# A graph layer's edge loop, its body thirty chunks long instead of six

## What is computed

```
h_fwd, h_rev = h @ W_forward.T, h @ W_reverse.T            # 64 numbers per node each
messages = h_fwd[src] * direction[:, 0:1] + h_rev[src] * direction[:, 1:2]
scores = leaky_relu(einsum('ef,hf->eh', messages, attn_forward[0]), 0.2)     # 4 heads
exp_scores = exp(scores - scores.max(axis=0))
norm = exp_scores / (segment_sum(exp_scores, dst)[dst] + 1e-10)
outs = [segment_sum(messages * norm[:, hd:hd + 1], dst) for hd in range(4)]
...
x = x + gnn(layernorm(x), edge_index, edge_attr_2, ...)
x = x + ffn(layernorm(x)[None], ...)[0]
```

## Time and profile before

| | |
|---|---|
| time, median of 3 runs | 2498.59 us (2497.01 to 2499.44) |
| the profiled execution | 2504.92 us, its span 2503.1 us |
| mean granted TensorE clock of it | 0.924 |
| busy PE, DVE, POOL | 2162.4, 1958.6, 1608.8 us |

### The profile page before, as it was taken

One profiled execution on the slowest core, in us unless ns is written; L12 is line 12 of the kernel. 1 busy time (PEld: TensorE's weight loads), 2 busy tenths in 40 slices (PEclk: granted clock), 3 DMA queues, 4 the chain that ended last, 5 costly groups with the idle time before them and its releaser, 6 DMA issues.

```text
span 2503.1 us, 46180 instructions
## 1 busy us (share of the span) xinstructions
PE 2162.4 (86%) x12873; PEld 1868.6 (75%) x12874; DVE 1958.6 (78%) x4609; ACT 357.4 (14%) x1034; POOL 1608.8 (64%) x1725
## 2 busy tenths in 40 slices
PE   7598989899898989999898999999946589999970
PEld 6487878778787877878787787878736478888870
DVE  5797888888788878888888887888848856666657
ACT  4100000000000000000000000000016434444435
POOL 6676767676676767667676766767746753333327
PEclk9699999999999999999999999999955599999995
DMA  6232222222222222223222222222245676666657
GB/s 206 58 69 61 68 61 67 61 67 63 61 67 61 67 60 67 62 61 67 61 67 61 67 63 61 68 61 67 61 133 164 215 215 200 197 199 199 199 168 266
DMA packets 175493, 259.46 MB, mean 104 GB/s; under 512 B 46538, under 2 KB 120479, under 8 KB 174972
## 3 DMA queue, kind: packets, MB, share of 16 engines
q0 software_dynamic: 52672, 119.37, 19.5%
q1 hardware_dynamic: 122556, 136.70, 18.0%
HBM read 218.01 MB, written 38.81 MB: 103 GB/s over the span
## 4 chain that ended last, share of the span: by engine, by line
PE 41%; DVE 31%; issue 16%; DVEq 6%; DMA 3%; SPq 1%; ACT 1%; POOL 1%; ACTq 0%; POOLq 0%
PE p_hot L1007 31%; PE p_win L902 5%; DVE hot_ex L1072 4%; DVE p_hot L1122 4%; DVE p_part L1040 4%; DVE rows L1037 3%; DVEq L1772 3%; DVE onehot L1109 2%; DVE rows L1127 2%; DVE p_y L1995 1%; PE p_y L1940 1%; PE p_h L1930 1%; DVE hid_t L1967 1%; DVE second L1975 1%; DVE back L1980 1%
## 5 line engine op out<-in xcount | busy, mean ns | idle before, releaser
L280 POOL DMA_INDIRECT rows<-node_table,index x1343 | 1278.6, 952 | 506.6 <-issue 398.3
L1007 PE MATMUL p_hot<-parts,onehot 128*128 128x476 f32 x6160 | 1403.5, 388 | 75.7 <-issue 58.0
L1007 PEld LDWEIGHTS p_hot<-parts,onehot 128*128 128x128 f32 x6160 | 1170.8, 192 | 280.9 <-issue 73.5
L1122 DVE SCALAR_TENSOR_TENSOR p_hot<-place_no,place_of_source,p_hot 128x476 f32<-128x476 f32 x440 | 293.1, 711 | 98.9 <-PE p_hot L1007 98.9
L902 PEld LDWEIGHTS p_win<-hot_ex,msg 128*65 128x65 f32 x3136 | 201.8, 143 | 116.6 <-issue 113.3
L902 PE MATMUL p_win<-hot_ex,msg 128*65 128x64 f32 x3136 | 210.9, 227 | 87.4 <-DVE hot_ex L1072 86.3
L956 ACT ACTIVATE p_dve<-score,neg_shift 128x64 f32<-128x64 f32 x98 | 31.2, 318 | 1718.1 <-DVE score L1057 1718.1
L1781 POOL DMA_INDIRECT expert_rows<-ys,back x104 | 102.3, 983 | 269.3 <-DVE ys L2000 146.3
L1109 DVE TENSOR_TENSOR onehot<-key,p_dve 128x896 fp32r<-128x896 f32 x220 | 237.3, 1079 | 36.2 <-PE p_hot L1007 32.9
L1127 DVE TENSOR_REDUCE rows<-p_hot 128x136 f32<-128x952 f32 x220 | 252.8, 1149 | 7.7
L1023 DVE TENSOR_TENSOR shared<-shared,p_win 65x64 f32 x784 | 170.2, 217 | 111.8 <-PE p_win L902 16.0
(11 more groups left out here) (269 smaller groups left out, 1422.2 us busy)
## 6 DMA issues: line engine op xcount, KB each, us to landing
shared<-in_w SPq DMA_DIRECT2D x120, 512.0 KB, 4.5
rows<-node_table,index POOLq DMA_INDIRECT x1343, 3.0
xs<-dispatched SPq DMA_DIRECT2D x104, 129.5 KB, 4.1
shared<-expert_rows SPq DMA_DIRECT2D x12, 896.0 KB, 8.1
key<-hot_keys SPq DMA_DIRECT2D x62, 128.0 KB, 3.0
token_rows<-in_x SPq DMA_DIRECT2D x7, 896.0 KB, 12.8
key<-hot_keys SPq DMA_DIRECT2D x32, 192.0 KB, 3.1
shared<-in_x SPq DMA_DIRECT2D x7, 768.0 KB, 9.1
```

The costliest lines, as they stand in the source:

```text
L280: pool.indirect_dma_start(out=rows[:, s, k, :], out_offset=None, in_=table, in_offset=bass.IndirectOffsetOnAxis(ap=index[:, s, 0, k:k + 1] ...
L1007: last = pe.matmul(p_hot[:, v, d, 0:PLACES * COLS], onehot[:, v, gr, :], parts[:, gr:NT:GP, m, d * COLS:(d + 1) * COLS], start=(gr == 0 an ...
L1122: last = dve.scalar_tensor_tensor(out=found[:, d], in0=place_no[:, :].unsqueeze(2).broadcast_to([P, PLACES, COLS]), scalar=place[:, ds(f, ...
```

## The change

One line is added. The body is five times as long and the number of turns follows from it: `BODY` is 30, `TURNS` is (98 - 6) // 30 = 3, and `LOOPED` is 2 + 90 = 92 as before.

More of the change, by code:

```diff
@@ L66 @@
     BODY += len(CYCLE)
+BODY *= 5
 TURNS = (NCH - 3 * RING) // BODY
```

## The result

The changed kernel takes 2430.13 us, median of 4 runs (2424.8 to 2431.6), against 2499.02 us before (4 runs beside them): a ratio of 0.972, 95% interval [0.970, 0.974], 68.9 us less. It lies in the range of 2408 to 2440 us, 11 us above the value forecast. The profiled execution of the changed kernel was the quickest of the four, 2424.8 us (span 2422.9); the one before was slower than most plain runs, 2504.9 us.

The account below looks back on a forecast made before the run. PE was taken to bound the kernel, stalling at each edge-loop turn's end. Twelve ends at 6.7 us, 80.4 us, less 1 us for POOL, give 79.4 us: 2419 us from a 2498.6 us median, range 2408 to 2440 us.

Parts of the forecast that it names:

- The price of an end: Edge loop, each end of a turn: costs 6.7 us; twelve taken branches go, 80.4 us in all.
- Its make-up: At each turn's end: 4.33 us of PE branch, 1.58 us of slow clock, the remainder DVE's refill.
- the rest of DVE's own refill: DVE's stall behind its loop branch: what is left of 6.7 us after 4.33 us and 1.58 us on PE.
- POOL's charge: POOL's gathers in the loop: 51.53 us per three chunks against 51.32, falling back 0.21 us; 1 us charged in all.
- the room of 2.1 us: Slack between a chunk's last gather and DVE's use of it, late in a turn: lasts ten groups of three chunks.
- one of the signs of being wrong: Edge loop: the forecast is wrong if, among other signs, chunks in mid-body run over 51.6 us a group of three.
- What lies ahead of it and behind it is the same: Stages outside the edge loop, which covers chunks 2 to 91 before and after: taken as unchanged.
- SP, ACT and POOL's longer code: Their loop branches, 45 to 53 ns: taken to refill nothing, 0 us; up to 8 us kept for the range.
- the likeliest range of 2414 to 2433 us: Whole kernel: ends at 6.6 to 6.8 us, up to 84 us gained; POOL takes 6.3 us, longer code 8 us.
- No gain: Rival listed first, edge loop: the stall belongs to code fetched, not the jump; time stays 2498.6 us; chance 0.02.
- Skipping forward: Second rival, PE's branch over wide windows (L991): far targets stall 6.7 us each; slower, 2519 us; chance 0.03.
- POOL's stalls at its code: Third rival, POOL in the loop: 45 code fetches at 1.05 us, 47 us, giving 2466 us; chance 0.07.

Follow-up runs that it names:

- the two profiles of before: The kernel before, profiled, then run and profiled again with no edit: spans 2503.1 and 2498.4 us, chunks 2 to 92 in 1633.6 and 1629.5 us.
- the fewer gathers: One gather less in every third loop chunk: 2423.0 us against the changed kernel's 2430.2; in the kernel with all chunks written out, 2392.4 us against 2418.8.

## Why the prediction was right, and where it was short

**The price of an end** was forecast at 6.7 us and twelve of them at 80.4 us. With 30 x 51.32 = 1539.6 us for the loop without ends, the two profiles of before give 94.0 / 14 = 6.7 and 89.9 / 14 = 6.4 us. The first of them was the one I had, and it was the dearer: 0.3 x 12 = 3 to 4 us of the shortfall. The mechanism held: ends on PE go, and each takes its stall and its slow clock along.

**Its make-up** holds in size, but its terms do not add up one by one. What I left for "the rest of DVE's own refill", 6.7 less 4.33 and 1.58, is 0.8 us, and with PE's stall gone it is 0.9 us. Taken away alone, with PE's stall still there, it gained nothing.

**POOL's charge** of 1 us was the step that was mis-sized; the fewer gathers put it at 2.8 to 6.0 us in the loop. The place was right, but two things in it were not. First the lag: I took PE's and DVE's pace from one group of three, 51.32 us. Over 27 chunks it is 51.23 us, so POOL's 51.53 us fall back 0.30 us a group and not 0.21, and the room of 2.1 us lasts seven groups and not ten. The long groups are indeed the eighth of a turn's ten. (The room itself is not exact: both gathers that it was read from lie behind POOL's loop, whose last branch starts at 1737.0 us, and 1.89 us and five chunks' drift make 2.2 us.) Then the price: I charged POOL's lag, 0.21 us a group. What came is a packet of code in the way of a gather that had no room left, 0.95 to 1.4 us of waiting on DVE, and in half of the cases a fall of PE's clock on top. So one of the signs of being wrong came true in both profiles, groups in mid-body over 51.6 us: 52.3 and 52.7 us in the first, 52.5, 53.4 and 53.5 us in the second, where the clock dips four times in the loop and not twice.

**"What lies ahead of it and behind it is the same"** failed by 3 us. The expert stage turns 23 times through code that had moved.

**SP, ACT and POOL's longer code** was taken at nothing and was nothing; the 8 us kept for the range were not needed. That the time lies in the range owes something to them, and that is luck: without them the likeliest range of 2414 to 2433 us would have ended at 2425 us, and their width covered costs that I had not seen.

Together: 3.6 us from the price, 2 to 5 from POOL, 3 from the experts are 8 to 12 us; the forecast was 79.4, the measured gain 68.9 and 70.7 us.

**The rivals.** No gain is out: code goes on being fetched in straight bodies, 94 packets between 240 and 1675 us in the changed kernel, and free groups run at 51.23 us.

```profile
q8 instruction: 94, 1.54, 0.4%
q14 instruction: 81, 0.66, 0.2%
```

By the Trainium skill, "Runtime: NRT & Kernel Launch" (Instruction fetch mechanics), crossing from one block of code to the next is mostly hidden; these groups agree with that. Skipping forward is out, by L992. POOL's stalls at its code, 45 of them, did not come: it waits for "issue" 0.3 us at every gather in the first profile, and over 1 us once in the second (1.2 us) and three times in each kernel with fewer gathers (1.7 to 2.1 us); what these are is open. (The rival's own count was too high: 82 gathers of 240 instructions are a third, 2 of 6 packets and not 3.) That POOL would be the next to be late was right for another reason. And of the first rival something is left: it is fetched code that delays a gather once the room is gone.

## What to carry to other kernels

Look in a loop for idle time that the profile can put down to nothing, divide it by the number of turns, and compare a group of iterations that holds a loop's end with one that doesn't: that difference was right here within 5% as the price of an end, and the gain of the whole kernel was 11 to 13% less than forecast. Then ask what used the pause to catch up: an engine that is a fraction of a per cent too slow shows nothing until the pause is gone, and with its room gone other delays come to light, here the packets of code. And expect that a short wait ahead of PE can cost the clock as well as its length: here it did in five of ten.

## What the runs showed of the hardware that I had not expected

- A wait of 2.0 us on PE in the midst of a busy loop was followed by a granted clock of 0.54, and 32 matmuls took 3.55 us instead of 2.05 to 2.10; behind one of 2.25 us they took 2.10 us.
- While a packet of code was fetched, the last of a gather's sixteen parts could land 0.5 to 2.2 us behind the fifteenth; without such a packet none in the loop came over 0.5 us behind it.
- With DVE's refill gone and PE's stall left, the dips of the clock at an end were 6.8 us long in all 14 ends; in the two profiles of before 5 and 6 of 14 were, the others 3.4 us.
- A loop can turn 0.13 us slower (of 15.85 us) by where its code lies. What in the place decides was not found: it changed with shifts of 20 and 26 instructions.
- The loop's taken branch cost PE 3.6 to 5.2 us, and DVE stood idle for 1.7 to 2.3 us behind its own, at each of the ends seen.
